# A Mamba stage in two halves of channels, each half's front work beside the other half's scan units, in a software-pipelined macaron block

## What is computed

```python
x = x + 0.5 * ffn(ln(x))            # router, top 6 of 32 experts, 96 wide, and a shared one of 192
n = ln(x)
h = n + mamba(rms(n))
x = x + (h + mlp(rms(h)))           # mlp of 1024, scaled by 0.5 in the kernel's sums
x = x + 0.5 * ffn(ln(x))

def mamba(h):                        # 512 channels, 16 states
    z, x, B, C, dt = split(h @ in_proj)
    dt = softplus(dt @ dt_proj + bias)
    x = silu(conv4(repeat(x)))
    for t in range(256):             # per channel and state
        state = exp(dt[t] * A) * state + dt[t] * x[t] * B[t]
        y[t] = sum_over_states(state * C[t])
    return ((y + x * D) * silu(z)) @ out_proj
```

## Time and profile before

| | us |
|---|---|
| median of 3 runs (1859.88 to 1867.7) | 1865.11 |
| the profiled execution | 1861.63 |
| its span, first to last instruction | 1859.8 |
| busy PE / DVE / ACT / POOL | 1578.5 / 1274.9 / 816.7 / 976.4 |
| mean granted TensorE clock | 0.939 |

### The profile page before, as it was taken

One profiled execution on the slowest core, in us unless ns is written; L12 is line 12 of the kernel. 1 busy time (PEld: TensorE's weight loads), 2 busy tenths in 40 slices (PEclk: granted clock), 3 DMA queues, 4 the chain that ended last, 5 costly groups with the idle time before them and its releaser, 6 DMA issues. The chain is left out here.

```text
span 1859.8 us, 24175 instructions
## 1 busy us (share of the span) xinstructions
PE 1578.5 (85%) x7088; PEld 1149.6 (62%) x7088; DVE 1274.9 (69%) x2124; ACT 816.7 (44%) x1644; POOL 976.4 (52%) x1048
## 2 busy tenths in 40 slices
PE   6879888776789897989989898898986999777879
PEld 5756555665676555755566566755664666556768
DVE  3435995589748994699748995589736984399521
ACT  4435443544355343554345353554344444444323
POOL 2522775256436672376625774367722884157525
PEclk9989999988899999999999999999997999789989
DMA  7853223332233222422224222332222323233333
GB/s 255 311 165 122 80 75 101 117 111 82 99 100 120 80 91 72 131 91 73 77 89 135 80 83 88 97 115 87 80 82 86 102 92 103 69 114 108 120 99 130
DMA packets 71911, 200.44 MB, mean 108 GB/s; under 512 B 9536, under 2 KB 22048, under 8 KB 71392
## 3 DMA queue, kind: packets, MB, share of 16 engines
q1 hardware_dynamic: 63584, 173.65, 28.4%
q0 software_dynamic: 8192, 25.17, 4.7%
HBM read 173.62 MB, written 23.59 MB: 106 GB/s over the span
## 5 line engine op out<-in xcount | busy, mean ns | idle before, releaser
L657 PE MATMUL gub<-x_hi,wr 128*128 128x512 f32 (+1 forms) x1040 | 430.3, 414 | 75.3 <-DVE hid L1026 56.7
L1293 POOL TENSOR_TENSOR hid<-hid,u_sb 128x512 f32<-128x512 f32 (+1 forms) x260 | 288.2, 1109 | 373.9 <-ACT u_sb L889 252.3
L738 PE MATMUL acc<-hid,w_down 128*128 128x512 f32 (+1 forms) x1040 | 409.8, 520 | 1.6 <-POOL hid L1293 1.6
L659 PE MATMUL gub<-x_hi,wr 128*128 128x512 f32 (+1 forms) x1040 | 375.2, 361 | 0.0
L658 PE MATMUL gub<-x_lo,wr 128*128 128x512 f32 (+1 forms) x1040 | 374.7, 360 | 0.0
L1314 POOL TENSOR_TENSOR ring<-ring 128x512 f32<-128x512 f32 x192 | 252.1, 1313 | 200.8 <-DVE ring L1195 199.8
L1189 DVE TENSOR_TENSOR_SCAN ring<-decays,side 128x512 f32<-128x512 f32 x256 | 310.9, 1215 | 18.7 <-ACT decays L989 11.0
L889 ACT ACTIVATE u_sb<-gub 128x512 f32<-128x512 f32 (+1 forms) x260 | 132.8, 511 | 418.6 <-PE gub L659 418.5
L657 PEld LDWEIGHTS gub<-x_hi,wr 128*128 128x128 f32 x1040 | 207.2, 199 | 119.6 <-issue 43.7
L899 ACT ACTIVATE hid<-gub 128x256 f32<-128x256 f32 (+1 forms) x324 | 156.5, 484 | 282.4 <-PE gub L659 197.3
L1301 POOL TENSOR_TENSOR hid<-hid,weight 128x512 f32<-128x512 f32 (+1 forms) x240 | 264.2, 1101 | 16.3 <-POOL hid L1293 3.3
(11 more groups left out here) (119 smaller groups left out, 1944.9 us busy)
## 6 DMA issues: line engine op xcount, KB each, us to landing
wr<-w_halves SPq DMA_DIRECT2D x234, 512.0 KB, 3.3
wm_gu<-in_w_mlp POOLq DMA_DIRECT2D x64, 256.0 KB, 3.0
w_halves<-wr SPq DMA_DIRECT2D x26, 512.0 KB, 4.9
wm_down<-in_w_mlp POOLq DMA_DIRECT2D x64, 128.0 KB, 2.6
w_raw<-in_w_gu SPq DMA_DIRECT2D x26, 256.0 KB, 4.9
rows<-parts SPq DMA_DIRECT2D x16, 384.0 KB, 2.3
cst<-rows SPq DMA_DIRECT2D x48, 128.0 KB, 2.9
xin<-in_x SPq DMA_DIRECT2D x8, 256.0 KB, 3.6
```

Of the source, the lines that this page charges most:

```text
L657: mm(out, w[:, 0, half, k, :], x_hi[:, k, a:b], start=(k == 0), stop=False)
L659: last = mm(out, w[:, 1, half, k, :], x_hi[:, k, a:b], start=False, stop=(k == KC - 1))
L738: last = mm(acc[k][:, a:b], w, h[:, a:b], start=(c == 0), stop=(c == (MLP_CHUNKS if mlp else FFN_CHUNKS) - 1))
L1293: nc.gpsimd.tensor_tensor(h, h, u_sb[c % USLOTS][:, a:b], ALU.mult).then_inc(sem["hidden"], 1)
```

## The change

The Mamba stage is cut into two halves of channels (groups 0 and 1; groups 2 and 3), and each half's front work gets buffers of its own, so that it may stand beside units.

- The first half's front (`front(0, ...)`) and the norms `lnA` and `rms1` of the next item are moved one step ahead, beside units 16 to 31 of the current item (`"next"`). Step 1 does its own (`"own"`, norms `lnO`, `rmsO`), since nothing was ahead of it; step 2 does its own and the next item's. From step 3 on a step begins with its units. Step 8 has no next item.
- The second half's front stands beside units 0 to 15, together with `ln1` and its routing; `ln2` stands beside units 16 to 31.
- Units are spread over the whole step, the MLP included, in `own` steps too.
- `sp`, `sp_dt`, `sp_x` and `y0` work on two groups at once, twice a step (before: `sp` on four, the others on one).
- `xpad`, `tmp`, `dtr`, `yg`, `hn_next` are new tensors of their own; `ubuf` and `lbuf` are halved; `WSLOTS` goes from 8 to 6. ACT copies `hn_next` to `hn` (`carry`). `bst` comes back from DRAM in two pieces, the second after all units of the step before (`b_rest`).
- Waits for "all of the step before" (`s.prior`) become waits at the place of the item in the list.

```diff
-WSLOTS, MSLOTS, HSLOTS, USLOTS = 8, 3, 4, 3
+WSLOTS, MSLOTS, HSLOTS, USLOTS = 6, 3, 4, 3
...
+def front(half, when):
+
+    if half:
+        return [("b_rest",)] + [(k, 1, when) for k in ("x", "dt")] + [("split", 2, when)] + [
+            (k, 1, when) for k in ("sp", "z", "sp_dt", "sp_x", "y0")]
+    return [("split", 0, when), ("x", 0, when), ("dt", 0, when), ("split", 1, when)] + [
+        (k, 0, when) for k in ("sp", "z", "sp_dt", "sp_x", "y0")]
...
+    late_front, next_front = 1 <= t <= 2, 2 <= t < BATCH
...
+    follow = norm("lnA") + norm("rms1") + merge(front(0, "next"), ln2, SPACE) if next_front else ln2
+    light = norm("lnO") + norm("rmsO") + front(0, "own") if late_front else []
+    begin = len(light)
+    light += merge(unit_items(0), front(1, "own") + ln1, SPACE)
+    light += merge(unit_items(1), follow, SPACE) if follow else unit_items(1)
+    light += [("yz", JC - 1), ("outp",)] + norm("rms2")
...
+        cut = begin + len(unit_items(0) + front(1, "own")) * 2 // 3
+        out = hand + keep + merge(chain, light[:cut], WEIGHT) + merge(ff[:-TAIL], light[cut:], WEIGHT) + ff[-TAIL:]
+    else:
+        heavy = mlp_items() + ahead + ff
+        out = hand + heavy[:6] + keep + merge(heavy[6:-TAIL], light, WEIGHT) + heavy[-TAIL:]
...
+WEIGHT = {"n1": 1, "n2": 1, "nm": 1, "rq": 0.75, "split": 2, "x": 4.5, "z": 1, "dt": 0.5, "sp": 1.7, "sp_dt": 1.7,
+          "sp_x": 0.9, "y0": 0.6, "ub": 2, "unit": 2, ("unit", UNITS - 1): 8, "rt1": 1, "yz": 0.4,
+          ("yz", JC - 1): 3, "outp": 3, ("n1", "rms2"): 3, ("n2", "rms2"): 3, ("nm", "rms2"): 2,
...
+          "g": 1.3, "u": 1.3, "down": 1.7, "gum": 1.7, "cmb": 0.2}
+SPACE = {"n1": 3, "n2": 3, "nm": 2, "rq": 0.75, "split": 4, "x": 5, "z": 2, "dt": 2, "sp": 2, "sp_dt": 2,
+         "sp_x": 1, "y0": 1, "ub": 2, "unit": 2, "rt1": 2, "yz": 0.1}
...
-        ubuf = sb("ubuf", [P, JC, SEQ])
-        lbuf = sb("lbuf", [P, JC, SEQ])
-        tmp = ring[:, 2, :, :]
-        dtr = ring[:, 3, 1, :]
...
+        yg = sb("yg", [P, JC, SEQ])
+        ubuf = sb("ubuf", [P, 2, SEQ])
+        lbuf = sb("lbuf", [P, 2, SEQ])
+        tmp = sb("tmp", [P, 2, SEQ])
+        dtr = sb("dtr", [P, SEQ])
+        xpad = sb("xpad", [P, 2, SEQ + TAPS - 1])
...
+                elif kind == "carry":
+                    act.wait_ge(sem["normed"], s.count("normed", it, 0))
+                    A(hn[:], hn_next[:], ACT.Copy).then_inc(sem["carried"], 1)
...
                 elif kind == "dt":
                     act.wait_ge(sem["side_filled"], s.count("side_filled", it, 1))
-                    if it[1] == 0:
-                        if (least := s.prior("y_sum")) is not None:
-                            act.wait_ge(sem["y_sum"], least)
-                        if (least := s.prior("decay")) is not None:
-                            act.wait_ge(sem["decay"], least)
+                    for last_read in ("dt_fix", "decay", "dtx"):
+                        if (least := s.count(last_read, it, 0)) is not None:
+                            act.wait_ge(sem[last_read], least)
...
-                    v.tensor_tensor(dtx[:, j], dtx[:, j], lbuf[:, j], ALU.add).then_inc(sem["dt_fix"], 1)
+                    v.tensor_tensor(dtx[:, of], dtx[:, of], lbuf[:], ALU.add).then_inc(sem["dt_fix"], 1)
...
-                    v.tensor_tensor(y[:, j], y[:, j], z2[:, j], ALU.mult).then_inc(sem["y_gated"], 1)
+                    v.tensor_tensor(yg[:, j], y[:, j], z2[:, j], ALU.mult).then_inc(sem["y_gated"], 1)
```

More of the change, by code:

```diff
@@ L145, in routing, with unit_items @@
     return [("rt1", call)] + [("rq", call, i) for i in range(len(ROUTE))]
-def unit_items():
+def unit_items(half):
     out = []
-    for u in range(UNITS):
+    for u in range(half * UNITS // 2, (half + 1) * UNITS // 2):
         j, p = u // PAIRS, u % PAIRS
@@ L155, in unit_items, with after @@
         out += [("yz", j - 1)] if p == 2 and j else []
-        out += [("sp_dt", j + 1), ("sp_x", j + 1)] if p == 3 and j + 1 < JC else []
-        out += [("y0", j)] if p == 4 else []
-    return out
+    return out
+def front(half, when):
[4 more added lines that the diff above has]
+        (k, 0, when) for k in ("sp", "z", "sp_dt", "sp_x", "y0")]
+def after(items, new, *befores):
+    at = max(items.index(b) for b in befores) + 1
+    return items[:at] + new + items[at:]
 def items_of(t):
@@ L174, in items_of @@
     keep += [("load", 0)] if following else []
-    norms = norm("lnA") + norm("rms1") if mamba else []
-    project = ([("split", 0), ("x", 0), ("dt", 0), ("split", 1), ("dt", 1), ("x", 1), ("sp",), ("split", 2),
-                ("z", 0), ("sp_dt", 0), ("sp_x", 0), ("z", 1)] if mamba else [])
-    units = unit_items() if mamba else []
-    last = [("yz", JC - 1), ("outp",)] + norm("rms2") if mamba else []
-    r0 = [("r0",)] if mamba else []
-    r0 += [("again",)] if t < 2 else [("shift",)] if t < BATCH else []
-    r0 += [("again_n",)] if 1 <= t < BATCH - 1 else []
+    turn = [("r0",), ("carry",)] if mamba else []
+    turn += [("again",)] if t < 2 else [("shift",)] if t < BATCH else []
+    turn += [("again_n",)] if 1 <= t < BATCH - 1 else []
     ln2 = norm("ln2") + routing("f2") if mlp and not own else []
@@ L188, in items_of @@
     ff = ffn_items(t)
-    along = norms + project
-    length = LENGTH if twin or first and second else SHORT
-    scan = r0 + (merge(units, ln2 + ln1, length) if units else ln2 + ln1) + last
+    if not mamba:
+        if t == 0:
+            return hand + keep + merge(ff[:-TAIL], turn + ln1, WEIGHT) + ahead + ff[-TAIL:]
+        return mlp_items() + ahead + norm("ln2a") + routing("f1") + [("rt2", "f1"), ("hx", "f1")] + ff
+    follow = norm("lnA") + norm("rms1") + merge(front(0, "next"), ln2, SPACE) if next_front else ln2
@@ L193, in items_of @@
+    light = norm("lnO") + norm("rmsO") + front(0, "own") if late_front else []
[3 more added lines that the diff above has]
+    light += [("yz", JC - 1), ("outp",)] + norm("rms2")
+    turns = [("end", "mlp")] if mlp else []
+    turns += [("nm", "lnO")] if late_front else []
     if not mlp:
-        return hand + keep + merge(ff[:-TAIL], along + scan, length) + ahead + ff[-TAIL:]
@@ L195, in items_of @@
-    if own:
+        out = hand + keep + merge(ff[:-TAIL], light, WEIGHT) + ahead + ff[-TAIL:]
+    elif own:
         chain = mlp_items() + ahead + norm("ln2a") + routing("f1") + [("rt2", "f1"), ("hx", "f1")]
-        if not mamba:
-            return chain + ff
-        return hand + keep + merge(chain, along, LENGTH) + merge(ff[:-TAIL], scan, LENGTH) + ff[-TAIL:]
-    heavy = mlp_items() + ahead + ff
-    return hand + heavy[:6] + keep + merge(heavy[6:-TAIL], along + scan, length) + heavy[-TAIL:]
@@ new lines, in items_of @@
+        out = hand + keep + merge(chain, light[:cut], WEIGHT) + merge(ff[:-TAIL], light[cut:], WEIGHT) + ff[-TAIL:]
+    else:
+        heavy = mlp_items() + ahead + ff
+        out = hand + heavy[:6] + keep + merge(heavy[6:-TAIL], light, WEIGHT) + heavy[-TAIL:]
+    out = after(out, turn, *turns)
+    if next_front:
+        at = out.index
+        assert at(("shift",)) < at(("n1", "lnA")) and at(("ub", UNITS // 2)) < at(("split", 0, "next"))
+        assert at(("yz", 1)) < min(at(("x", 0, "next")), at(("z", 0, "next")))
```

196 lines of the change are left out of this document (98 added, 98 removed).

## The result

| | before | after |
|---|---|---|
| median, us | 1863.7 (4 runs, 1859.88 to 1867.7) | 1843.76 (4 runs, 1834.36 to 1847.6) |
| profiled execution, us | 1861.63 | 1842.69 |
| busy DVE / ACT / POOL, us | 1274.9 / 816.7 / 976.4 | 1276.3 / 842.0 / 982.9 |

A forecast was written before the change was run, and what follows sets the result against it. PE and DVE were taken to bound different stretches. Terms -24 (steps 3 to 5), -8 (6), 0 (7), -34 (8), +18 (2), -5 (1) gave -53 us, 1808.6 against 1861.6; median forecast 1812 us, range 1752 to 1868.

The forecast's parts named there:

- Steps 3 to 6: Steps 3 to 5 at 207 us for 215, step 6 likewise 8 us less; -32 us in all.
- at the 92% of today's units 85 us: First part of steps 3 to 5 (units 0 to 15): DVE's 78.6 us of work at 92% busy takes 85 us.
- second rival: Gain only in step 8; PE waits on shared `side` banks, steps 3 to 6 stay: some 1848 us, chance 0.17.
- second part: Units 16 to 31 of steps 3 to 5: PE sets the pace, 85 us of work at 0.88, 97 us.
- Step 2: Carries its own first front and the next item's; 210 us for 191, 18 more.
- Step 8: Units fill the opening chain and the first front is gone: 155 us for 189, 34 less, the largest term.
- Step 7: Opening chain 65 us (69 before), the rest 148 us: 213 for 212, no change.
- Step 1: Start 14 us earlier, units with the second front 130 us for 120: 4 to 5 us less.
- The POOL exclusion: DVE work wholly in SBUF beside units waits about 1.0 us for a running POOL instruction; 8 us a step taken.
- third rival: Slower: all 30 newly exposed DVE instructions a step pay 1.0 us for the POOL exclusion; 1916 us, chance 0.13.
- Slots and `carry`: Six weight slots and the extra ACT copy of 0.63 us were taken to cost nothing.
- First rival: DVE's spread frees PE in full: both parts of steps 3 to 6 at 0.93; 1756 us, chance 0.20.

The follow-up runs named there:

- experiment 1: Convolution item cut into five pieces: in the kernel after, 1843.6 us (0.9899); in the kernel before, 1848.7 us (0.9929).
- Experiment 4: Kernel after with the first front moving ahead one step later, so step 3 carries the doubled front: 1849.83 us (0.9933).
- experiment 3: Kernel after, two variants: no units or front beside the chain in steps 7 and 8, 1855.26 us; no front moved ahead, 1888.4 us.
- experiment 5: Six of seven POOL unit additions cut to 16 of 256 columns: kernel after 1793.89 us (0.9624), kernel before 1823.65 us (0.9791).
- experiment 2: Kernel before with `WSLOTS` 6 in place of 8, nothing else: 1860.36 us (0.9994).
- experiment 6: Each unit's second DVE multiplication cut to 16 of 256 columns: kernel after 1786.5 us (0.9589), kernel before 1780.85 us (0.9563).

## Why the prediction was right and wrong

**Steps 3 to 6: forecast -32 us, measured -10.0. The step that failed is "at the 92% of today's units 85 us".** The work was counted rightly: DVE's 78.6 us measured 78.50, and of PE's 73 us in the first part, 77. But the 92% was DVE's share in a stretch without front work. The forecast carried it over to a stretch in which the same three banks also serve the second front, and it put PE's wait for a bank at nothing. With one bank more, steps 3 to 6 take 205.9, 207.7, 208.4 and 196.6 us, 818.6 in sum; forecast were 817, measured in after 839.1, in before 849.1. In the kernel before, the same bank gives nothing (852.7). This is the mechanism of the second rival, "banks `side` are now shared by front and units, and PE waits there", which had a chance of 0.17 and a price of 1848 us, the nearest of all cases to the 1843.76 measured. It is shown for the four steps together. From the step's begin to its seventeenth scan, the four take 359.7 us in sum in after, 356.2 and 361.2 in the two kernels with the same code there, and 347.0 with four banks, with DVE busy for the same time. So the bank gives 9 to 14 us in the first parts and 5 to 8 behind them. But steps 3 to 5 still need 88 to 90 us for the first part, DVE at some 88%: the 85 us aren't reached, and that the whole comes to 817 is luck in part.

The prediction's sum for the second part has a slip as well: 15 chunks of 4.5 us are 67 us and not 66. In step 5 PE's work there is 83 us for the 85 forecast, at 0.84 of the time for the 0.88 assumed, so the two errors hide each other in 98 for 97 us.

The conv item shows inside this as the next limit. The timeline of step 5 after, its second part, DVE, then ACT, then PE (start us, duration, what, and in brackets the idle time before):

```profile
1077.50 1.43 DVE L1158 TENSOR_SCALAR xs<-xpad,vecs 128x256 f32<-128x256 f32 x2 [1.72 <-ACT xpad L975]
1078.86 2.45 DVE L1162 SCALAR_TENSOR_TENSOR xs<-xpad,vecs,xs 128x256 f32<-128x256 f32 x6
1082.00 0.69 DVE L1166 SCALAR_TENSOR_TENSOR xs<-tmp,xs 128x512 f32<-128x512 f32 x1 [0.70 <-ACT tmp L981]
1082.61 0.68 DVE L1064 SCALAR_TENSOR_TENSOR hid<-hid,gub 128x512 f32<-128x512 f32 x1
```

```profile
1073.56 0.57 ACT L938 ACTIVATE hid<-gub 128x512 f32<-128x512 f32 x1
...
1081.34 0.63 ACT L981 ACTIVATE tmp<-xs 128x512 f32<-128x512 f32 x1 [3.96 <-DVE xs L1162]
```

```profile
1083.34 0.79 PE L695 MATMUL gub<-x_hi,wr 128*128 128x512 f32 x1 [4.98 <-DVE hid L1064]
```

The gating (L1064) needs the tanh of its chunk, which ACT has done by 1074.13 us (L938), and stands behind the item in DVE's list until 1082.61. PE, whose next product needs the bank that it frees, stands still for 4.98 us and starts again at half clock: the granted clock is 0.50 (1.2 GHz) from 1083.3 to 1086 us, and L695 takes 0.79 us, 0.40 before. The prediction saw ACT's wait for the taps and costed it at nothing, since "it did so before, ahead of fewer units". The trace of after has 16 such waits of ACT, 60.5 us together and 5.7 at the longest; the one of before has 16 too, 52.4 us and 3.4. So the waits are hardly longer, and what is new is what stands behind them. ACT's idle time is not time of the kernel: the pieces gave back 12 us with four banks, 8 in step 7 (5 with step 8), and nothing alone, and part of what they give goes into the longer taps of experiment 1.

**Step 2: forecast +18, measured +26.6.** The term that was off is the start. It was to come 12 us earlier; the first scan came 53.1 us after the step's begin, where it had come after 57.8. These 7 us are nearly the whole miss. Just ahead of it PE waits for the transfer that brings the C rows back. That the units reach it before it has landed because one front fewer lies between is my reading of it, not tested:

```profile
355.01 0.61 PE L870 MATMUL side<-bst,sel_b 96*128 96x256 bf16 x2 [6.35 <-DMA cst<-rows]
```

The 152 us behind it came out at 147, by luck: they were reckoned from 142.7 us of DVE's work at a share of 94%, for which no row stands (before has 109.27 of 121 us, 90%), while DVE had 60.17 + 64.41 us, 85%, and the clock was 0.80 and 0.87. A sum 18 us too high and a share too high cancelled. Experiment 4 gives the size of the doubled front: without it step 2 is at 197.2, so 21 of the 27 us are its price.

**Step 8: forecast -34, measured -38.2.** The times are right, term by term: chain 65 us, measured 60; rest 75, measured 73; tail 15, measured 17. For the chain this is luck in part: 60 us of DVE's work at 92% were assumed, and the windows show 47.59 in 59 us, 81%. In the rest the share held (66.41 of 74 us, 90%; forecast 91%). By the table of experiment 3, 18.3 us of the gain come from the absent front and 19.9 from the units (and the second front) beside the chain. What the prediction didn't see is that the second depends on the first: with the own front in place, the units beside the chain are worth 2.5 us. Work moved ahead is also a loan: 11 us of PE's work leave step 8, 10 of them stand again in step 2, and that step pays 26.6.

**Step 7: forecast 0, measured +8.2.** The chain came out at 63 us for 65, with 11 scans in it (10.7 assumed), but DVE had 50.60 us in it at 80%, where 60 at 92% were assumed: here too work and share were both too high. The rest was put at 148 us, PE's work at 0.94, and took 158. With the conv items in pieces it takes 150, so the item is the cause of nearly all of it; 3 of these 8 us come back in step 8.

**Step 1: forecast -5, measured -0.8**, and step 0 another -3.9. The first scan of step 1 comes 10.3 us earlier (54.4 us after its begin, before 64.7; forecast 14), and the end comes hardly earlier.

**The POOL exclusion: forecast +8 us of DVE a step, measured about none.** DVE's busy time is the same in both kernels, 1274.9 and 1276.3 us. The single lines of after (ns, min/median/max), against the earlier trace rows:

```profile
L1162 DVE SCALAR_TENSOR_TENSOR xs<-xpad,vecs,xs x96: 471/476/1580, 140.7 to 1594.5; 128x256 f32<-128x256 f32 x96
```

```profile
L1196 DVE TENSOR_TENSOR dts<-dtx,dts x16: 691/1652/1668, 156.5 to 1660.8; 128x512 f32<-128x512 f32 x16
```

The argument that POOL starves in a run of taps held: the median tap pays nothing, and only 2 of these 96 take over 0.9 us. Cut into pieces, where the taps are no longer one run, 25 do (experiment 1). The mean is 0.49 us, below the 0.55 to 0.7 forecast; the two first taps of each item (L1158) have 0.60. The wide `dts` product still pays 1.0 us, as the narrow one did, but 16 times and not 32. The third rival falls: experiment 5 moves both kernels alike. The rule of the Trainium skill, page "SBUF — State Buffer", section "Who interferes with whom", agrees with these rows; it says who waits, and not how often they meet, and the forecast of 8 us a step hung on that.

**Slots and `carry`.** Nothing, as forecast: experiment 2, and no wait of PE for a transfer into `wr` among the waits of either kernel. The second `sp` and `carry` lengthen ACT's busy time by 25 us; none of PE's larger waits is for them.

**First rival** (1756 us): it would have needed PE's share in both parts at 0.93; in step 5 PE's work is 0.83 and 0.84 of the two parts.

**Signs.** Of those that the prediction named, three held: units start within 10 us (the first product of steps 3 to 6 comes after 5.5 to 8.6 us, though its scan, behind the conv item, only after 12.6 to 16.0), DVE is under 85% in the second part (75% in step 5), step 8 is near 155 us. DVE near 92% in the first part, step 2 near 210 us and the mean of the taps failed, and PE waits on `side` banks in the first part, as the second rival has it.

**What stays open.** How the rest of steps 3 to 6 and of step 2 divides between the item, the clock's half-speed stretches and PE's order. Also whether a product bank could be freed in another way: the four-bank kernels show what it would bring (29 us), but not how.

## What to carry to other kernels

When work is moved beside other work, don't carry over the busy share that the bottleneck engine had; ask first which small set of buffers both now take from, and count how long each holds one, since an in-order engine stands behind the first that isn't free. An indivisible item with several exchanges between engines should be cut before it is moved into a busy stretch, but it pays only where nothing shorter is the limit, and an instruction that was safe in a row of its own kind may pay once others stand between (25 of 96 taps here). Moving a stage one step ahead in a pipeline saves at its end and costs at its start; cost the doubled step at the fill as carefully as the saving.

## What the hardware showed that was not expected

Cutting POOL's additions short, with DVE's instructions unchanged in number and size, makes DVE 36.6 us (before) and 43.6 us (after) less busy and the kernels 40 and 50 us faster. So the additions of an engine at 52%, which hardly appears among the waits of PE or DVE, cost this kernel over 2% of its time. One way is the exclusion that the earlier trace rows show once. By experiment 6 a microsecond of DVE is worth 0.7 and 0.5 us, so the shorter busy time explains an estimated 26 of the 40 us and 22 of the 50. The rest may be POOL's own latency; no run parts the two.

Cutting a run of DVE instructions apart can bring the exclusion in: the same 96 taps have a mean of 0.49 us as a run, and of 0.71 us in pieces beside the units.
